# A gram kernel's feature buffer laid out slot by slot instead of sample by sample

## What is computed

```
e = jnp.stack([tbl_0[ids[:, 0]], ..., tbl_25[ids[:, 25]]], axis=1)
all_emb = jnp.concatenate([bottom_output[:, None, :], e], axis=1)   # [2048, 27, 128]
gram = jnp.einsum('bfd,bgd->bfg', all_emb, all_emb)
z = gram[:, _TRIU_I, _TRIU_J]                                       # 351 products
h = jnp.concatenate([z, r_bottom_output], axis=1)                   # 479 columns
h = jnp.maximum(h @ W_top1 + b_top1, 0.0)                           # 512
h = jnp.maximum(h @ W_top2 + b_top2, 0.0)                           # 256
y = h @ W_top3                                                      # 1
```

## Time and profile before

| | us |
|---|---|
| three timed runs | 648.59, 648.86, 652.58 (median 648.86) |
| profiled execution, span | 643.8 |
| PE matmul busy | 395.4 (61%) |
| ACT busy | 310.4 (48%) |
| POOL busy | 285.1 (44%) |
| VectorE (DVE) busy | 235.1 (37%) |

### The profile page before, as it was taken

One profiled execution on the slowest core, in us unless ns is written; L12 is line 12 of the kernel. 1 busy time (PEld: TensorE's weight loads), 2 busy tenths in 40 slices (PEclk: granted clock), 3 DMA queues, 4 the chain that ended last, 5 costly groups with the idle time before them and its releaser, 6 DMA issues.

```text
span 643.8 us, 13317 instructions
## 1 busy us (share of the span) xinstructions
PE 395.4 (61%) x5324; PEld 296.7 (46%) x5324; DVE 235.1 (37%) x472; ACT 310.4 (48%) x470; POOL 285.1 (44%) x282
## 2 busy tenths in 40 slices
PE   2686572353578947625367894733536799467487
PEld 2464461232466835214256673412325578335375
DVE  3574560033286411030347822002135782202451
ACT  2484660056489512223559751412456983028832
POOL 7777357556003754664600573555550067250000
PEclk9798785565699987756568998955556899677689
DMA  5558442111224411111123441111121331010000
GB/s 157 165 184 230 168 139 58 38 40 44 91 98 134 144 41 43 45 47 36 49 81 109 152 126 29 51 42 43 41 68 57 132 114 50 25 42 6 8 4 0
DMA packets 21925, 50.39 MB, mean 78 GB/s; under 512 B 7288, under 2 KB 7320, under 8 KB 21744
## 3 DMA queue, kind: packets, MB, share of 16 engines
q1 hardware_dynamic: 12902, 30.96, 14.5%
q0 software_dynamic: 8832, 18.11, 10.6%
q10 hardware_dynamic: 138, 0.52, 0.2%
HBM read 49.00 MB, written 0.01 MB: 76 GB/s over the span
## 4 chain that ended last, share of the span: by engine, by line
PE 37%; issue 25%; another core or an unknown queue 13%; DMA 11%; ACT 9%; DVE 3%; SPq 0%; ACTq 0%; DVEq 0%
DMA table_raw<-in_tbl 11%; PE gram L442 11%; PE acc L421 5%; PE turned L403 5%; PE acc L422 4%; PE acc L449 4%; PE acc L451 4%; PE acc L450 3%; ACT pairs L559 3%; ACT table_hi L596 2%; DVE table_lo L716 2%; ACT features L577 1%; PE acc L509 1%; DVE onehot L732 1%
## 5 line engine op out<-in xcount | busy, mean ns | idle before, releaser
L368 POOL DMA_INDIRECT rows<-in_tbl,index x276 | 284.4, 1030 | 292.3 <-PE turned L403 157.0
L442 PE MATMUL gram<-features 128*26 128x26 f32 x4096 | 94.9, 213 | 151.8 <-issue 150.1
L421 PE MATMUL acc<-onehot,table_hi 125*128 125x512 f32 (+1 forms) x288 | 127.1, 441 | 50.2 <-DVE table_lo L716 22.7
L442 PEld LDWEIGHTS gram<-features 128*26 128x26 f32 x4096 | 70.7, 128 | 185.6 <-issue 183.3
L577 ACT COPY features<-turned 128x512 f32<-128x512 f32 (+2 forms) x80 | 82.2, 1062 | 139.4 <-remote 102.7
L422 PE MATMUL acc<-onehot,table_lo 125*128 125x512 f32 (+1 forms) x288 | 121.6, 422 | 0.0
L732 DVE TENSOR_SCALAR onehot<-wanted,row_number 125x512 fp32r<-125x512 int32 (+1 forms) x252 | 104.2, 475 | 33.7 <-PE acc L422 20.1
L557 DVE COPY aside<-gram 10x320 f32<-10x320 f32 x21 | 15.5, 737 | 234.6 <-remote 177.2
L421 PEld LDWEIGHTS acc<-onehot,table_hi 125*128 125x128 f32 x288 | 60.9, 211 | 71.8 <-issue 38.4
L559 ACT COPY pairs<-gram 18x128 f32<-18x128 f32 (+3 forms) x172 | 67.2, 390 | 1.5
L422 PEld LDWEIGHTS acc<-onehot,table_lo 125*128 125x128 f32 x288 | 60.9, 211 | 10.8
(11 more groups left out here) (40 smaller groups left out, 302.1 us busy)
## 6 DMA issues: line engine op xcount, KB each, us to landing
table_raw<-in_tbl SPq DMA_DIRECT2D x35, 500.0 KB
wanted<-in_onehot_ids SPq DMA_DIRECT2D x36, 256.0 KB
rows<-in_tbl,index POOLq DMA_INDIRECT x276
aside<-in_w SPq DMA_DIRECT2D x1, 1280.0 KB
bottom<-in_xT SPq DMA_DIRECT2D x4, 256.0 KB
h<-in_w SPq DMA_DIRECT2D x1, 512.0 KB
table_raw<-in_tbl ACTq DMA_DIRECT2D x1, 500.0 KB
pairs<-aside SPq DMA_DIRECT2D x16, 20.0 KB
```

The costliest lines, as they stand in the source:

```text
L368: pool.indirect_dma_start(out=rows[:, q % RING, f, :], out_offset=None, in_=gathered[f], in_offset=bass.IndirectOffsetOnAxis(ap=index[q // ...
L421: pe.matmul(to, table_hi[0:ROW_PARTS, i % TABLE_RING, c, :], of, start=(c == 0), stop=False)
L442: last = pe.matmul(gram[at:at + GRAM, q % 2, i // 4, 0:GRAM], features[:, q, i, 0:GRAM], features[:, q, i, 1:SLOTS], start=True, stop=True)
```

## The change

The dimensions of `features` are put in another order. Before, a partition held [tile of block, sample, slot], so a sample's 27 floats were adjacent. Now it holds [slot, tile of block, sample]: a slot has the 512 floats of the block's samples in a row, and the floats of one sample lie 512 floats (2 KB) apart. The buffer's size is the same, 55,296 floats per partition. The five places that use it follow: both operands of the gram matmul, ACT's copy of turned groups, ACT's copy of a small table's result, and VectorE's fill of slot 0.

```
-        features = sb("features", [P, BLOCK_TILES, P, SLOTS])
+        features = sb("features", [P, SLOTS, BLOCK_TILES, P])
...
                     last = pe.matmul(gram[at:at + GRAM, q % 2, i // 4, 0:GRAM],
-                                     features[:, q, i, 0:GRAM], features[:, q, i, 1:SLOTS], start=True, stop=True)
+                                     features[:, 0:GRAM, q, i], features[:, 1:SLOTS, q, i], start=True, stop=True)
...
                 nc.scalar.copy(
-                    features[:, q % BLOCK_TILES, :, 1 + first:1 + first + size].rearrange("d b f -> d f b"),
+                    features[:, 1 + first:1 + first + size, q % BLOCK_TILES, :],
                     turned[:, n % 2, 0:size, :]).then_inc(turned_out, 1)
...
-                    nc.scalar.copy(features[:, 0:samples.stop // P, :, slot].rearrange("d q b -> d (q b)"),
+                    nc.scalar.copy(features[:, slot, 0:samples.stop // P, :].rearrange("d q b -> d (q b)"),
                                    acc[:, i % 2, samples]).then_inc(acc_out, 1)
...
-                dve.tensor_copy(features[:, :, :, 0].rearrange("d q b -> d (q b)"), bottom[:]).then_inc(slot0_ready, 1)
+                dve.tensor_copy(features[:, 0, :, :].rearrange("d q b -> d (q b)"), bottom[:]).then_inc(slot0_ready, 1)
```

## The result

The changed kernel takes 710.86 us (median of 4 runs, 699.57 to 715.17) beside 648.73 for the kernel before: 1.085 times as long, with an interval of 1.077 to 1.093. Two of the four runs are slow ones, so the ratio compares the two fast runs (699.57 and 708.67) with the fast runs of the kernel before. The forecast of 643 us had the wrong sign, and the time lies above the range of 636 to 685.

A forecast was written before the change was run, and what follows sets the result against it. The prediction took waits between engines, stage by stage, as the bound. Span 643.8 - 8.5 (copies) + 2.5 (gram reads) = 637.8 us; the profiled run stands 5.1 us under the median, so 643 us, own range 638 to 648, full range 636 to 685.

The forecast's parts named there:

- (a): ACT's copies L577 and L627 write adjacent floats, 0.70 us instead of 1.20; gain 8.5 us, bounds 0 and 12.
- Rival 3: Nothing moves: reads hidden, ACT's saved time waited away because POOL's gathers pace much of the gram; 649 us, chance 0.14.
- (b): VectorE's fill of slot 0, four copies, can only become shorter; costed at 0, at most 0.5 us gained each.
- (c): TensorE's gram reads floats 2 KB apart: about 12.2 ns per pair at either clock; cost 2.5 us, lower bound 0.
- rival 1: TensorE's strided gram read doubles the pair at either clock, 23.4 ns instead of 11.7; 664 us, chance 0.26.
- Rival 2: TensorE's four samples in flight share one path in the gram, a pair costs 44 ns; 706 us, chance 0.15.

The follow-up runs named there:

- padded: Changed kernel with 4 floats of padding behind each slot, so a sample's floats lie 2064 bytes apart instead of 2048; ratio 1.008 to the kernel before.
- writes_only: Changed kernel, but the gram reads both operands from the constant tile `identity`, not `features`; 646.46 us beside 649.19 for the kernel before, ratio 0.994.
- before_again: The kernel before, unchanged, run again for its trace on a chip of the 463 us kind; ratio 1.001 to the kernel before.
- after_again: The changed kernel (2048-byte steps), run again for its trace on a chip of the 463 us kind; ratio 1.153 to the kernel before.

## Why the prediction was wrong

- *The copies (a).* The durations were forecast at 0.70 us and came to 0.57 to 0.59 where nothing disturbs them. The gain was sized at 8.5 us and is about 4: I counted every shorter copy on a chain as won, and did not ask what arrives next: the table loads and the transposes, whose waits grew. Rival 3 had this effect, and it took about half of the term, but its reason was POOL's gathers. Those don't explain the chips with 463 us, where the gain is as small.
- *VectorE's fill (b).* Its copy fell from 0.68 to 0.42 us, and the rows of L442 name no wait for it, as the 0 of the sum had it.
- *The read (c), as a price per float.* Right in size where the step is not a bad one: 12.2 ns per pair at either clock was forecast from ACT's write and the output layer, and padded measured 13. A lone stream showed the same at 50.7 ns (4 x 12.2 = 49). Some of this is luck, since no run shows that ACT's write and TensorE's read pay for the same thing. The pace of 8.8 ns that I started from at the full clock was itself misread: it came from a long burst, and bursts of 32 start a pair every 7.3 ns.
- *The read (c), at 2048 bytes.* Here the prediction failed. The step "fed at 1.7 ns a pair takes about 12.2 ns" took ACT's 108 bytes as standing for any distance. The kernel's step is a multiple of 256 bytes, and pairs took 34 to 35 ns (medians at the half and the full clock) in bursts of 32, some 28 ns more than before on the other chip, and 21 to 36 in longer ones. The sum has +2.5 us for this term; the changed kernel against writes_only, 1.085 less 0.994 of 649, makes it some 59 us, the delays of ACT and VectorE included.
- *What such a pace costs.* I let 0.4 us per burst be hidden, from the 0.46 us that the earlier trace rows show. In truth the whole pause can be filled: 256 pairs in a row take 7.39 us, no more than two bursts with their pauses took (2 x 3.73). So rival 1, whose 23.4 ns is near the pace of the long bursts, had the wrong place for its cost: it lies in the short bursts between transposes and in the waits for ACT.
- *Nobody else is touched.* This was not written down as a step, but it stands in the sum: only instructions that use `features` were priced. The cast of 7.67 us, the copies of the regrouping on ACT and VectorE, and with them the wait of 4.84 us, belong to instructions that never see `features`. Rival 2 came closest, with 706 us, and with its sentence that the streams share a path. But 44 ns for every pair is not what happened: the streams share at bad steps alone (13 ns at 2064 bytes), and at these a pair takes 25 ns in long bursts and 34 to 37 in short ones. That its number agrees is in part luck, since the delays of ACT and VectorE stand where it counted TensorE's.
- *The test that I named* did its work: the rest of the gram, the last 470 pairs, was to take over 15 us if the prediction was wrong. It took 17.5 (337.0 to 354.5), 5 of them waiting for ACT. L442's mean grew by 82 ns instead of 20 or less, and the three stretches between the gram stages became longer, although the copies became shorter.

One thing in the section on the change has to be put right: the buffer has 13,824 floats, or 55,296 bytes, per partition, not 55,296 floats. No number of the prediction rests on it.

## What to carry to other kernels

When a layout makes TensorE read one float here and one there, look at the step between them before its size: here 256, 512 and 2048 bytes were bad, and 16 bytes of padding on top of 2048 (less was not tried) took nearly all of the loss away. Or put two neighbours side by side, which here made both the writes and the reads nearly as cheap as adjacent ones. Price such a change not only on the instructions that touch the buffer but on every engine that uses the memory at the same moment, and look in the trace for instructions of a known length that suddenly last as long as somebody else's burst. And when a shorter instruction stands on a chain, name what arrives next before counting the gain.

## What the hardware showed

- Step and rate: TensorE's four column groups, each reading 26 + 26 floats per pair, ran at 7.3 ns per pair (full clock; 11.8 at the half) on adjacent floats in bursts of 32, 13 ns in steps of 16 or 2064 bytes at either clock, 16 in steps of 64 and 34 to 37 in steps of 256, 512 and 2048 (medians). In longer bursts the bad steps took 21 to 36.
- An engine can be held: a cast of 1.05 us on ACT, from one SBUF buffer to another, took 7.67 us while TensorE read in steps of 2048 bytes. The Trainium skill, page "SBUF — State Buffer", section "Who interferes with whom", says that TensorE and ACT never wait on anyone. The trace shows a longer cast, and the measurement decides. The six casts beside the gram took 1.05 to 1.11 us in before_again and 3.2 to 7.1 in after_again. One stream in such steps hardly held it (1.10 us), four did.
- ACT writes 512 floats from PSUM in 1.20 us at steps of 108 bytes, in 0.64 us in runs of two, in 0.57 to 0.59 us in runs of four and more.
- Small matmuls can be bound by what I read as the arrival of their instructions: 256 instructions each 3.73 us, at either clock, in the earlier trace rows. The traces support the reading: where the bursts of the earlier trace rows have 127 or 128 pairs, the instruction queue moves one packet of 16,384 bytes per burst, the packets start 3.5 to 4.3 us apart, and the next burst starts 1.3 to 1.5 us after a packet has ended. Slower matmuls fill that pause for nothing.
- The same program takes 463 us on some chips and 649 on others. In the latter TensorE trickles while POOL issues gathers; its idle time before L442 was 151.8 us there and 42.1 us in before_again. What those chips lack isn't known.
